# A scan layer with mixture of experts on one core: the weight-building stage is merged into the front, its diagonals written to DRAM by transfers

## The reference

```
h  = layernorm(x);  xn = norm(h) * gamma + beta;  xz = xn @ W_in.T
x_ssm, z = silu(causal_conv4(xz[:1024]) + conv_b), xz[1024:]
xp = x_ssm @ W_xproj.T;  B, C = xp[1:17], xp[17:33];  dt = softplus(xp @ W_dt.T + b_dt) + 0.001
A  = -exp(A_log)
dA = exp(A*dt);  dB = (1-dA)/(A+1e-8) * B;  h = clip(dA*h + dB*x, -10, 10)      # step by step over 4096 tokens
y  = sum_n C*h + D*x_ssm;  x = x + (y * silu(z)) @ W_out.T
x  = x + shared(layernorm(x)) + gated expert part + bias
```

## Time and profile before

| what | us |
|---|---|
| three runs of the kernel | 4498.34, 4503.36, 4510.58 (median 4503.36) |
| the profiled execution, its own time | 4499.18 |
| its span, first to last instruction | 4497.4 |
| setup, until the front's first load is issued | 0 to 48.59 |
| front | 48.59 to about 1076 |
| scan | about 1076 to 3531 |
| last stage | 3534 to 4497 |

### The profile page before, as it was taken

The page is one execution under the profiler, slowest core; times in us unless marked ns, Lnnn a source line. Parts: engine busy times, 40 slices in busy tenths (PEclk is TensorE's granted clock), DMA queues, the critical chain, the costliest instruction groups (busy, mean ns, idle before and its releaser), DMA issues. The chain is left out here.

```text
span 4497.4 us, 48927 instructions
## 1 busy us (share of the span) xinstructions
PE 4214.5 (94%) x14186; PEld 2452.6 (55%) x14186; DVE 3671.7 (82%) x4320; ACT 3169.2 (70%) x5820; POOL 3132.2 (70%) x1548
## 2 busy tenths in 40 slices
PE   2999999995999999999999999999999479999999
PEld 1777777773444444444444444444444157777777
...
GB/s 185 195 203 203 193 198 210 209 203 197 155 191 190 163 169 191 191 162 168 191 189 162 170 191 191 162 170 191 191 163 159 147 152 156 169 161 160 158 157 30
DMA packets 579687, 786.69 MB, mean 175 GB/s; under 512 B 101312, under 2 KB 304448, under 8 KB 577880
## 3 DMA queue, kind: packets, MB, share of 16 engines
...
...
## 5 line engine op out<-in xcount | busy, mean ns | idle before, releaser
L965 POOL TENSOR_TENSOR q<-g,cc 128x1024 f32<-128x1024 f32 x1024 | 2393.6, 2369 | 138.9 <-DVE g L1105 121.1
L1105 DVE TENSOR_TENSOR_SCAN g<-dd,carry,ps_a 128x512 f32<-128x512 f32 x2048 | 2400.0, 1255 | 37.5 <-ACT ps_a L987 24.4
L1045 PE MATMUL ps_y<-q,w_s 128*128 128x512 f32 x4096 | 2098.9, 593 | 20.0 <-POOL q L965 11.4
L987 ACT ACTIVATE ps_a<-dt_s,small 128x512 f32<-128x512 f32 x2048 | 1502.2, 734 | 5.4 <-DVE g L1105 5.4
L976 ACT ACTIVATE dd<-ps_d 128x512 f32<-128x512 f32 x2048 | 1287.9, 629 | 74.3 <-PE ps_d L1032 49.2
L1032 PE MATMUL ps_d<-dm,xk 99*128 99x512 f32 x2048 | 1103.6, 540 | 62.6 <-DMA dm<-band_d 25.5
L1032 PEld LDWEIGHTS ps_d<-dm,xk 99*128 99x128 f32 x2048 | 383.9, 188 | 1240.8 <-ACT dd L976 985.0
L1045 PEld LDWEIGHTS ps_y<-q,w_s 128*128 128x128 f32 x4096 | 777.2, 191 | 168.7 <-issue 49.7
L353 POOL TENSOR_TENSOR xnt_lo<-xnt_f,xnt_hi 128x512 fp32r<-128x512 f32 x64 | 110.3, 1723 | 562.4 <-ACT xnt_hi L378 562.4
L499 PE MATMUL ps_r_f<-xnt_hi,w_hi 128*128 128x512 f32 x1024 | 418.4, 409 | 13.8 <-DVE w_lo L672 13.8
L499 PE MATMUL ps_r_f<-xnt_lo,w_hi 128*128 128x512 f32 x1024 | 403.3, 394 | 0.0
(11 more groups left out here) (160 smaller groups left out, 4442.8 us busy)
## 6 DMA issues: line engine op xcount, KB each, us to landing
w_s<-w_d SPq DMA_DIRECT2D x256, 512.0 KB, 3.8
...
xt_d<-xt_f SPq DMA_DIRECT2D x256, 256.0 KB, 3.0
cc<-c_d SPq DMA_DIRECT2D x128, 512.0 KB, 11.4
...
xs_d<-xs_f SPq DMA_DIRECT2D x128, 256.0 KB, 2.6
zs_d<-zs_f SPq DMA_DIRECT2D x128, 256.0 KB, 2.9
...
```

The lines of the kernel that those rows point to most:

```text
L965: pool.tensor_tensor(q[:, s % QB:s % QB + 2, :], g[:, s % GB:s % GB + 2, :], rows, ALU.mult).then_inc(s_q, 2)
L987: act.activation(ps_a[:, s % AB, :], dt[:, blk % DTB, :], ACT.Exp, scale=small[:, blk % MD, S_A + n:S_A + n + 1]).then_inc(s_a, 1)
L1045: pe.matmul(ps_y[:, blk % 2, :], w[:, half % WB, at:at + P], q[:, s % QB, :], start=(n == 0), stop=(n == NS - 1)).then_inc(s_n, 1)
L1105: dve.tensor_tensor_scan(g[:, s % GB, :], dd[:, m % 2, n, :], ps_a[:, s % AB, :], carry[:, m, n:n + 1], ALU.add, ALU.mult).then_inc(s_g, 1)
```

## The change

The setup stage is gone; its work is spread over the front, and four transfers of the scan's start with it.

- **Loads.** SP begins with `x`, then `A_log`, gamma and beta (semaphore `s_gb`), then `W_in` in four quarters with a semaphore each (`s_wq`), then the other weights. PE's transposes wait for the identity alone; ACT rounds a quarter when it is there, between the passes over `x`; PE's first projection waits for the remainder of a quarter just before it uses it.
- **Small work.** `exp(A_log)` is ACT's first instruction; DVE's steps on it come after the remainders, in a slice of the tile `conv`. PE transposes `inv` after the fourth projection of chunk 0 (`turn_inverse`); DVE copies the result after `norm(1)` and SP stores it to a tensor of its own, `invt_d`. The small columns stay in SBUF (`small`).
- **Diagonals and bands.** In each of the chunks 0 to 3 SP issues one `clear_band` and two `clear_diagonal`: zeros from a tile of 132 columns, in runs of 528 and 512 bytes, about 3.2 MB a chunk. In each of the chunks 4 to 11 `fill_diagonal` writes the 2048 nonzero elements of one block, 4 bytes each, from `inv`. In chunk 12 the band of the scan's chunk 0 is filled. All of them stand between `store_b` and `store_zs(ch, 6)`.
- **Gather.** The 256 elements for `ba_d` are gathered at the end of the front.
- `xnt_f` has one buffer instead of two; in chunk 0 a slice of `conv` is the second.

The diff, cut to its core:

```diff
--- before.py
+++ after.py
-            setup(nc, sb, sem, t_in, ident, ones, minus_half, margin, within, xs_d, xp_d, xt_d, bt_d, band_d, w_d)
-            front(nc, sb, sem, t_in, ident, ones, minus_half, margin, within, clips, xs_d, dt_d, zs_d, xp_d, xt_d, bt_d, c_d)
-        scan(nc, sb, sem, ident, clips, xs_d, dt_d, xp_d, xt_d, bt_d, band_d, c_d, w_d, y_d, ba_d)
-        ffn(nc, sb, sem, t_in, ident, minus_half, xs_d, zs_d, xp_d, w_d, y_d, out)
...
-def setup(nc, sb, sem, t_in, ident, ones, minus_half, margin, within, xs_d, xp_d, xt_d, bt_d, band_d, w_d):
...
-                    ins.then_inc(s_dve, 1)
-                    dve.wait_ge(s_dve, done[0])
-                dve.wait_ge(s_exp, 1)
...
-                    step(dve.tensor_tensor(w[:, e, W_DIAG:W_DIAG + NS * P].rearrange("p (n k) -> p n k", n=NS),
-                                           bcast(ident[:, :], [(0, NS), (1, P)]),
-                                           bcast(inv[:, m, :], [(1, NS), (0, P)]), ALU.mult))
-                    step(dve.tensor_copy(w[0:NS, e, W_INVT:W_INVT + P], ps[:, m, :]))
...
-                    dve.sem_inc(s_w, 1)
...
-        xnt = sb("xnt_f", [P, 2, CH], c=c)
+        xnt = sb("xnt_f", [P, CH], c=c)
+        zeros, inv = sb("zeros", [P, ZEROS], c=c), sb("inv", [P, MD, NS], c=c)
...
+        raw_win = [t[:, h * XHALF:(h + 1) * XHALF, :].rearrange("p m t -> p (m t)") for t in (v, lg) for h in range(2)]
+        a_log, ea, ap_, an = (conv[:, 1, bass.ts(i, MD * NS)].rearrange("p (m n) -> p m n", n=NS) for i in range(4))
...
+        def plain(ch, q):
+
+            return conv[:, 0, :] if ch == 0 and q % 2 else xnt[:, :]
...
+                def clear_band(e, h):
+
+                    sp.dma_start(band_d[e, h, 0:1, :].rearrange("o (j n) -> o j n", n=ZEROS),
+                                 bcast(zeros[0:1, 0:1], [(0, BAND // ZEROS), (1, ZEROS)])).then_inc(s_zero, 16)
+                    sp.dma_start(band_d[e, h, 1:CH + 1, :].rearrange("(p s) n -> p (s n)", p=P).rearrange("p (j n) -> p j n", n=ZEROS),
+                                 bcast(zeros[:, 0:1], [(0, SUB * BAND // ZEROS), (1, ZEROS)])).then_inc(s_zero, 16)
+
+                def clear_diagonal(m):
+
+                    sp.dma_start(w_d[m, :, :].rearrange("p (n k) -> p n k", k=P),
+                                 bcast(zeros[:, 0:1], [(0, NS), (1, P)])).then_inc(s_zero, 16)
+
+                def fill_diagonal(m):
+
+                    whole = w_d[m, :, :]
+                    sp.dma_start(bass.AP(tensor=whole.tensor, offset=whole.offset, ap=[(NS * P + 1, P), (P, NS)]), inv[:, m, :],
+                                 allow_slow_non_contiguous=True).then_inc(s_diag, 16)
+
+                def fill_first_band():
+
+                    for h in range(2):
+                        sp.dma_start(band_d[0, h, :, 0:2 * NS], bt_d[h, 0, 0:CH + 1, :],
+                                     allow_slow_non_contiguous=True).then_inc(s_diag, 16)
...
                 load_x(0)
-                for stage, at in ((v, 0), (lg, KD // 2)):
-                    sp.dma_start(stage[:, :, :].rearrange("p m t -> p (m t)").rearrange("p (k n) -> p k n", n=2 * DI),
-                                 t_in["W_inT"][at * P:(at + KD // 2) * P, :].rearrange("(k p) n -> p k n", p=P))\
-                        .then_inc(s_wt, 16)
+                for dst, src in ((a_log, t_in["A_log"].rearrange("(m p) n -> p m n", p=P)),
+                                 (gamma[:, :], t_in["ln_gamma"]), (beta[:, :], t_in["ln_beta"])):
+                    sp.dma_start(dst, src).then_inc(s_gb, 16)
+                for k in range(KD):
+                    sp.dma_start(raw_win[k], t_in["W_inT"][k * P:(k + 1) * P, :]).then_inc(s_wq[k], 16)
...
                 for r in range(3):
...
-                sp.wait_ge(s_lo, 3)
+                load_x(1)
+                sp.wait_ge(s_pool, 1)
+                clear_edges()
+                sp.wait_ge(s_lo, KD + 1)
...
-                load_x(1)
...
+                    if ch == 0:
+                        sp.wait_ge(s_ivt, 1)
+                        sp.dma_start(invt_d.rearrange("n m p -> n (m p)"), raw_invt).then_inc(s_diag, 16)
...
@@ -321,6 +281,17 @@
                     store_zs(ch, 5)
                     store_turned(ch, 5)
                     store_b(ch)
+                    if ch < 4:
+                        clear_band(ch // 2, ch % 2)
+                        clear_diagonal(2 * ch)
+                        clear_diagonal(2 * ch + 1)
+                    elif ch < 4 + MD:
+                        if ch == 4:
+                            sp.wait_ge(s_zero, 16 * EDGES)
+                        fill_diagonal(ch - 4)
+                    elif ch == 4 + MD:
...
                 sp.wait_ge(s_xpo, CHUNKS * 32)
+                for b in range(BATCH):
+                    gather_ahead(b)
+                sp.wait_ge(s_diag, 16 * (MD + 3 + BATCH))
...
+                        if ch > 0:
+                            act.wait_ge(s_xl, ch * KD + q)
+                        elif q >= 2:
+                            act.wait_ge(s_xl, q - 1)
+                        for dst in (plain(ch, q), xnt_hi[:, ch % 2, q, :]):
...
+                def upper_win(k):
+
+                    act.wait_ge(s_wq[k], 16)
+                    act.activation(w_hi[:, k, :], raw_win[k], ACT.Copy).then_inc(s_hi, 1)
+
+                act.wait_ge(s_gb, 48)
+                act.activation(ea, a_log, ACT.Exp).then_inc(s_ea, 1)
+                upper_win(0)
+                scale_xnt(0, 0)
+                scale_xnt(0, 1)
+                upper_win(1)
+                scale_xnt(0, 2)
+                scale_xnt(0, 3)
+                upper_win(2)
+                upper_win(3)
+                act.wait_ge(s_wt, 9 * 16)
...
+                            if ch == 0:
+                                pe.wait_ge(s_lo, q + 1)
...
+                    else:
+                        pe.wait_ge(s_ivt, 1)
...
+                def turn_inverse():
+
+                    pe.wait_ge(s_set, SETUP)
+                    for m in range(MD):
+                        last = pe.transpose(ps_t[0:NS, m // 4, (m % 4) * P:(m % 4 + 1) * P], inv[:, m, :], ident[:, :])
+                    last.then_inc(s_ivm, 1)
...
+                def lower_win(k):
+
+                    dve.wait_ge(s_hi, k + 1)
+                    dve.tensor_tensor(w_lo[:, k, :], raw_win[k], w_hi[:, k, :].bitcast(F32), ALU.subtract).then_inc(s_lo, 1)
...
+                dve.tensor_scalar(ap_, ea, -1.0, 1e-8, ALU.mult, ALU.add).then_inc(s_set, 1)
...
+                dve.reciprocal(inv[:, :, :], ap_).then_inc(s_set, 1)
...
+                dve.wait_ge(s_set, SETUP)
+                dve.wait_ge(s_xl, KD)
...
+                    if ch == 0:
+                        dve.wait_ge(s_ivm, 1)
+                        dve.tensor_copy(raw_invt, ps_t[0:NS, 0:2, :].rearrange("p b t -> p (b t)")).then_inc(s_ivt, 1)
...
-                fill_band(0)
-                sp.dma_start(small[:, :, :], w_d[:, :, W_BIG:W_COLS].rearrange("m p s -> p m s"),
-                             allow_slow_non_contiguous=True).then_inc(s_sm, 16)
                 load_x(0, 0)
-                sp.wait_ge(s_band, 32)
...
-                for b in range(BATCH):
-                    gather_ahead(b)
-                sp.wait_ge(s_ba, 16 * BATCH)
                 load_ahead(0)
...
-                    sp.dma_start(raw_inv[NS * r:NS * (r + 1), :, :], w_d[:, 0:NS, W_INVT:W_INVT + P]
-                                 .rearrange("m n p -> n m p")).then_inc(s_wt[0], 16)
+                    sp.dma_start(raw_inv[NS * r:NS * (r + 1), :, :], invt_d).then_inc(s_wt[0], 16)
```

More of the change, by code:

```diff
@@ L176, in front @@
-def front(nc, sb, sem, t_in, ident, ones, minus_half, margin, within, clips, xs_d, dt_d, zs_d, xp_d, xt_d, bt_d, c_d):
+            front(nc, sb, sem, t_in, ident, ones, minus_half, margin, within, clips, small, xs_d, dt_d, zs_d, xp_d, xt_d, bt_d, c_d,
+                  band_d, w_d, invt_d, ba_d)
+        scan(nc, sb, sem, clips, small, xs_d, dt_d, xt_d, bt_d, band_d, c_d, w_d, y_d, ba_d)
+        ffn(nc, sb, sem, t_in, ident, minus_half, xs_d, zs_d, xp_d, invt_d, y_d, out)
+def front(nc, sb, sem, t_in, ident, ones, minus_half, margin, within, clips, small, xs_d, dt_d, zs_d, xp_d, xt_d, bt_d, c_d,
+          band_d, w_d, invt_d, ba_d):
@@ L217, in front @@
         S = lambda n: sem("f_" + n, c)
-        s_wt, s_x, s_one, s_hi, s_lo, s_b1 = S("weights"), S("x"), S("one"), S("hi"), S("lo"), S("b1")
+        s_wt, s_x, s_one, s_hi, s_lo = S("weights"), S("x"), S("one"), S("hi"), S("lo")
+        s_wq = [S(f"wq{k}") for k in range(KD)]
+        s_gb, s_pool, s_ea, s_set = S("gb"), S("pool"), S("ea"), S("set")
+        s_ivm, s_ivt, s_zero, s_diag = S("ivm"), S("ivt"), S("zero"), S("diag")
         s_st, s_pow, s_xn, s_tr, s_te, s_xl = S("stats"), S("pow"), S("xn"), S("tr"), S("te"), S("xl")
@@ L778, in scan @@
         S = lambda n: sem("s_" + n, c)
-        s_sm, s_band, s_ba = S("small"), S("band"), S("ba")
```

(1 more changed line is left out.)

199 lines of the change are left out of this document (67 added, 132 removed).

## The result

| | median, us | runs |
|---|---|---|
| before, beside the changed kernel | 4500.85 (4497.82 to 4510.58) | 4 |
| changed | 4535.92 (4533.49 to 4537.01) | 4 |

The ratio is 1.0074, with a 95% interval of 1.0062 to 1.0086. The forecast was 4459, and its range ended at 4483. The profiled execution of the changed kernel has a span of 4534.0 us against 4497.4, at a mean clock of 0.973 against 0.981.

The account below looks back on a forecast made before the run. Front full with PE, scan with POOL and DVE, so time was only at the seams. Terms -65.3 + 1.0 + 30.0 + 1.0 - 2.2 + 0.5 - 9.0 gave -44.0: median 4503.4 to 4459.4 us, 8-in-10 range 4431 to 4483.

Parts of the forecast that it names:

- The start: Front's start: SP issues x at about 0.7, the second projection ends at 36.1 against 101.4; -65.3 us.
- The rest: Remaining edits: one xnt_f buffer, longer inverse runs in the last stage, diagonal rows of 8192 bytes; 0 each.
- has air: Scan's queue: said to have room at a share of 0.63, so the changed diagonal rows cost 0 (-3 to +3).
- the sign of it: Scan or last stage: differing by over 5 us elsewhere would mean a cause not seen.
- Pitch of 8192 bytes: Scan: diagonal rows of 8192 instead of 8836 bytes cost 0 (-3 to +3).
- The zeros: Chunks 0 to 3: 3.18 MB of zeros ahead of x take 10.6 us each and delay later chunks; +30.0 us.
- small transposes: Front: PE's eight small transposes now lie on the path, as PE is full; +1.0 us (0.9 to 1.9).
- The margins: Front: time between x landing and its use, 3.3 us for chunk 2 and 0.1 for chunk 3.
- The elements: Chunks 4 to 11: 2048 four-byte writes each, 1 to 1.5 us, absorbed by pauses of 2.2; +1 in all.
- The second seam: Front to scan: first band and small columns go, -2.2; gathers at front's end +0.5; gather out of scan -9.0.
- B: Rival: zeros are dear, 212 GB/s or slower; 48 or more in place of 30, 4477 to 4495; chance 0.13.
- C: Rival: slower, above 4503, if 4-byte writes cost over 11.5 us a chunk; 0.04 with the like.

Follow-up runs that it names:

- e_pad: The changed kernel with 32 unused bytes in front of the scan's tile cc, putting the shifted tiles back on multiples of 64; 4483.5 us, ratio 0.9967.
- b_off: The kernel before with 32 unused bytes in front of cc, moving the scan's tiles to 32 above a multiple of 64; 4555.8 us, ratio 1.0123.
- e_late: The changed kernel with clears and fills issued at the end of a chunk, behind the load of x and the last stores; 4495.9 us, ratio 0.9985.
- e_nofill: The changed kernel without the eight transfers that write the diagonals' 2048 nonzero elements each; 4527.0 us, ratio 1.0061.

## Why the prediction was wrong

- **The start**: right, -65.3, and by its own steps (30.3 for the last quarter, 36.65 for the second projection).
- **The failed step: "The rest", and with it the scan "as long as before otherwise".** The prediction counted what the change does to instructions and transfers of the scan. It did not ask where the tiles lie once `small` is allocated outside. e_pad and b_off show that this alone is worth 49 to 51 us in the scan. It was costed at nothing because it was not seen; that the queue "has air" at a share of 0.63 is an average: at the start of a chunk it is full (1.02 from 1250 to 1270), and 50 us over 16 chunks are 3 us each. The prediction had named the sign of it: a scan that differs by over 5 us elsewhere means a cause not seen. It differed by 55.2.
- **Pitch of 8192 bytes, 0 (-3 to +3)**: with the addresses put right, about 6 us of the scan remain, and a pitch of 8832 removes them; by medians it isn't certain.
- **The zeros, +30.0 with the small transposes' +1.0: 42.8.** The delay by the zeros was nearly right: 10.6 was put, and against e_late it is 10.7 to 11.4. The margins were right too: in chunk 1 the load is issued 12.6 us late (1.2 of it stay in e_late, without the zeros; the small transposes are among it) and takes 0.4 longer to land; 13.0 less the margin of 3.3 is 9.7, and chunk 1's period grew by 9.7. The step that failed is the 2.2 us a chunk, 8.8 in all, that DVE's pauses were to absorb. The pauses of 1.10 and 1.07 did go in chunk 1, but two later ones, 0.50 and 0.35 before, grew to 2.71 and 1.93, and the next load was issued no earlier for it. That 300 GB/s came near is partly luck: the rate is 199 in the window of the 528-byte runs and 345 in that of the 512-byte runs, and the nearest row was of reads. Of the Trainium skill's rule (DMA: Bandwidth & Descriptors, Specifications: line rate from 512 bytes on) the runs say: nearly, where the runs of 512 bytes begin on multiples of 64 in DRAM (345 GB/s, against 385 in runs of 2 KB), and no, where they don't (145).
- **The elements, +1: 5.2**, and e_nofill takes 5.4 off that stretch. The same 2.2 of pauses were counted on here; without them the 1 to 1.5 a chunk of the estimate would have been 8 to 12.
- **The second seam**: the gathers at the front's end cost 4.6, not 0.5, because they queue behind the last stores of dt and the stage can't end before they land. The gather out of the scan gave 5.4 of 9.0. The loads of C follow at once, as told, but the first of them takes 12.6 us to land, on a queue that is now busy, and POOL waits 5.22 us for it, not 2.4.
- **Rivals**: none held. B (the zeros dear, 48 or more) was nearest in its place. C, the slower one, had its price in the elements, and mis-summed it: 44 us undo the gain, not 74, or about 7.7 a chunk instead of 11.5. The elements measured 0.7. None of the rivals had a cost in the scan beyond its start.
